# Attention and low-rank FFN on one core: the split of the softmax row sums between GpSimd and VectorE, 864/160 columns before, 896/128 after

## The reference

```python
x = x + layernorm(attention(layernorm(x)))     # 16 heads of 64 features, 2048 queries and keys
x = x + layernorm(ffn(layernorm(x)))           # x U1 (128x32), V1 (32x512) + b1, gelu, U2, V2 + b2
# attention, for every head:
q, k, v = x @ Wq + bq, x @ Wk + bk, x @ Wv + bv
out = softmax(q @ k.T / 8, axis=-1) @ v        # 2048 x 2048 probabilities a head
y = concat(out) @ Wo + bo
```

## Time and profile before

| | |
|---|---|
| median of three runs | 2367.11 us |
| the profiled execution | 2369.93 us, its span 2368.1 us |
| granted TensorE clock, mean | 0.991 of full speed |
| TensorE busy | 98% of the span |
| GpSimd busy | 92% |
| VectorE busy | 89% |
| ACT busy | 57% |
| DMA | 63.24 MB, 27 GB/s |

### The profile page before, as it was taken

One profiled execution on the slowest core, in us unless ns is written; L12 is line 12 of the kernel. 1 busy time (PEld: TensorE's weight loads), 2 busy tenths in 40 slices (PEclk: granted clock), 3 DMA queues, 4 the chain that ended last, 5 costly groups with the idle time before them and its releaser, 6 DMA issues.

```text
span 2368.1 us, 43238 instructions
## 1 busy us (share of the span) xinstructions
PE 2329.5 (98%) x15228; PEld 1191.7 (50%) x15228; DVE 2118.1 (89%) x3388; ACT 1355.7 (57%) x1610; POOL 2185.3 (92%) x1220
## 2 busy tenths in 40 slices
PE   8999999999999999999999999999999999999898
PEld 4455555555545555545555554554554555544444
DVE  7898999999999998999999999999999999888877
ACT  6655555555555656555555555555555565655545
POOL 6999999999999999999999999999999999989986
PEclk8999999999999999999999999999999999999998
DMA  2001001000000000100110000100000000110101
GB/s 60 25 17 29 29 15 33 29 15 28 29 19 28 29 24 19 33 27 17 29 31 17 28 29 15 33 29 15 28 29 21 27 29 24 27 33 24 37 23 36
DMA packets 88762, 63.24 MB, mean 27 GB/s; under 512 B 54661, under 2 KB 72453, under 8 KB 88549
## 3 DMA queue, kind: packets, MB, share of 16 engines
q1 hardware_dynamic: 87684, 60.21, 8.7%
q10 hardware_dynamic: 864, 0.26, 0.1%
HBM read 56.88 MB, written 2.61 MB: 25 GB/s over the span
## 4 chain that ended last, share of the span: by engine, by line
PE 90%; POOL 4%; DVE 3%; issue 1%; DMA 1%; ACT 1%; SPq 0%; POOLq 0%; DVEq 0%; ACTq 0%
PE o_ps L485 36%; PE spare_ps L440 14%; PE score_ps L464 10%; PE score_ps L470 9%; PE score_ps L467 9%; POOL total L1274 3%; PE spare_ps L408 3%; PE spare_ps L417 3%; PE spare_ps L426 3%; PE spare_ps L530 3%; DVE max_part L948 1%; DMA m_all<-m_scratch 1%; DVE ln_stats L920 0%; PE spare_ps L510 0%; SPq L1470 0%
## 5 line engine op out<-in xcount | busy, mean ns | idle before, releaser
L1274 POOL TENSOR_TENSOR total<-total,probs 128x864 f32<-128x864 f32 (+1 forms) x896 | 1822.1, 2034 | 142.7 <-ACT probs L757 32.7
L757 ACT ACTIVATE probs<-score_ps 128x1024 f32<-128x1024 f32 x1024 | 993.2, 1022 | 860.1 <-PE score_ps L470 860.1
L948 DVE TENSOR_REDUCE max_part<-spare_ps 128x1 f32<-128x512 f32 x2028 | 1294.9, 680 | 178.5 <-PE spare_ps L440 162.8
L485 PE MATMUL o_ps<-probs,v_sb 128*64 128x512 f32 x4096 | 982.1, 600 | 0.0
L485 PEld LDWEIGHTS o_ps<-probs,v_sb 128*64 128x64 f32 x4096 | 266.4, 137 | 447.6 <-issue 295.9
L440 PE MATMUL spare_ps<-k_hi,q_hi 64*128 64x512 f32 x2028 | 465.1, 451 | 10.8 <-DVE kd_lo L1133 5.6
L440 PEld LDWEIGHTS spare_ps<-k_hi,q_hi 64*128 64x128 f32 x2028 | 198.0, 184 | 463.3 <-issue 218.4
L464 PE MATMUL score_ps<-q_hi,kd_hi 64*128 64x512 f32 x2048 | 414.1, 398 | 5.1 <-ACT score_ps L747 5.1
L470 PE MATMUL score_ps<-q_hi,kd_lo 64*128 64x512 f32 x2048 | 408.6, 391 | 0.0
L467 PE MATMUL score_ps<-q_lo,kd_hi 64*128 64x512 f32 x2048 | 407.6, 390 | 0.0
L991 DVE TENSOR_REDUCE part_sum<-probs 128x160 f32<-128x640 f32 (+1 forms) x255 | 334.2, 1311 | 1.8 <-ACT probs L757 1.8
(11 more groups left out here) (150 smaller groups left out, 1268.4 us busy)
## 6 DMA issues: line engine op xcount, KB each, us to landing
m_all<-m_scratch SPq DMA_DIRECT2D x64, 512.0 KB, 3.6
denom<-denom_scratch SPq DMA_DIRECT2D x122, 128.0 KB, 2.9
m_scratch<-neg_rows SPq DMA_DIRECT2D x256, 1.0 KB
denom_quarters<-row_turned SPq DMA_DIRECT2D x224, 4.0 KB, 1.8
y_acc<-in_L_attn_x SPq DMA_DIRECT2D x8, 256.0 KB, 6.0
key_f<-in_L_attn_x SPq DMA_DIRECT2D x8, 256.0 KB, 3.0
block_out<-probs SPq DMA_DIRECT2D x8, 256.0 KB, 2.3
denom_scratch<-denom_col SPq DMA_DIRECT2D x61, 4.0 KB, 3.3
```

The costliest lines, as they stand in the source:

```text
L485: last = nc.tensor.matmul(o_ps[half(h), :], v_sb[:, b, kt, half(h)], probs[:, st % RING, h, :], start=(kt == 0), stop=(kt == T - 1))
L757: nc.scalar.activation(probs[:, st % RING], score_ps[st % 2][:], ACT.Exp, scale=SCALE).then_inc(s["exp_done"], 1)
L948: nc.vector.reduce_max(max_part[:, G % 2, h, qt, kc:kc + 1], bank[max_bank(n, h)], AX.X).then_inc(s["max_done"], 1)
L1274: nc.gpsimd.tensor_tensor(others(total[:, G % 2], G), so_far, others(probs[:, st % RING], G), ALU.add).then_inc(s["sum_done"], 1)
```

## The change

The constant that says how many of the 1024 columns VectorE takes goes from 160 to 128. So GpSimd adds 896 columns in each tile in place of 864, in chunks 0 to 62, and VectorE's reductions and merges of these chunks have 128 columns. The last chunk, the order of all instructions and all waits stay as they are.

```diff
-SHARE, GROUP = 160, 4
+SHARE, GROUP = 128, 4
```

## The result

The changed kernel takes 2411.88 us (median of four runs, 2409.80 to 2413.55). The kernel before takes 2365.67 us (median of four, 2364.19 to 2367.35). The ratio is 1.0200 with a 95% interval of 1.0185 to 1.0216, so the change costs 46.2 us, 2.0%. The forecast was 2414 us, with a range from 2400 to 2426.

A forecast was written before the change was run, and what follows sets the result against it. TensorE was taken to set the loop's pace, with GpSimd 99% taken and becoming the pace. 67.1 us of added adds, less 19.5 idle and 0.5 for VectorE, gave 47 us: 2414 us for the median, range 2400 to 2426.

The forecast's parts named there:

- GpSimd's reserve and the pace: Main loop: GpSimd has only 1.15 us a period to spare, so it becomes the pace at 143.6 us a period.
- The price of a column: GpSimd's adds: 32 more columns cost 0.071 us each, 67.1 us over 945 adds (bounds 56.7 to 71.4).
- The idle time taken up: GpSimd's present waits absorb 15.2 us in the loop and 4.3 us near the end, 19.5 together.
- Where TensorE is held: At output projection L530, TensorE waits for GpSimd's normalisation L1061, some 40 us in sum.
- The ring: Rival: only the eight probability tiles bind, exponentials waiting for adds; 9 us come free, 2405 us; 9%.
- VectorE's relief: Narrower reductions and merges take 72 us off VectorE's busy time, worth nothing for the end time except 0.5 us.
- The end: From chunk 59 to the last, the end moves with GpSimd, so the last chunks' growth counts in full.
- Start-up: GpSimd's wait ahead of the first add is start-up and takes up none of the added work.
- The sum: Whole kernel: 67.1 - 19.5 = 47.6 us, less 0.5 for VectorE, 47 us; 2414 us for the median.
- clock rival: TensorE's new waits lower its clock once a chunk: 56 us more, 2470 us; 7%.
- hidden: Rival: GpSimd's free time or shrinking gaps between adds absorb the whole 67.1 us, no change, 2367 us; 5%.
- VectorE: Rival: L440's waits for VectorE's maxima set TensorE's pace; at most 72 us come back, 2295 us; 4%.

The follow-up runs named there:

- 144: VectorE 144 columns, GpSimd 880, half of the change, against the kernel before (160/864): 16.0 us slower, ratio 1.0056 to 1.0084.
- gp_alone: GpSimd adds 896 columns as in the change, VectorE's four-tile reductions keep 160: 2409.50 us, 45.8 us slower than the kernel before.
- short_norm: The changed kernel with the normalisation L1061 multiplying only 8 of 512 columns: 2363.57 us against 2363.70 for the kernel before.
- late_projection: The changed kernel with output projection L530 in a chunk's fourth double step, not the second: 2410.70 us, 47.2 us slower than the kernel before.
- ve_alone: The kernel before with VectorE's four-tile reductions cut to 128 columns, GpSimd keeping 864: 2362.27 us against 2363.70.
- share152: VectorE 152 columns, GpSimd 872, against the kernel before (160/864): 1.1 us slower, ratio 0.9996 to 1.0018.
- late_share: The kernel before with 192/832 columns (VectorE/GpSimd) in chunks 56 to 62 only: 2361.87 us against 2363.50.
- 168: VectorE 168 columns, GpSimd 856, against the kernel before (160/864): 1.4 us slower, ratio 0.9999 to 1.0023.
- ve_norm_late: The changed kernel with VectorE doing L1061 to chunk 55, behind the second double step's maxima, and L530 in the fourth: 2502.97 us, 137.7 us slower than before.
- 192/832: VectorE 192 columns, GpSimd 832, against the kernel before (160/864): 14.3 us slower, ratio 1.0048 to 1.0078.
- ve_norm: The changed kernel with VectorE doing normalisation L1061 for chunks 0 to 55 in the same double step: 2543.71 us, 179.9 us slower than the kernel before.

## Why the prediction was right, and where it was off

*GpSimd's reserve and the pace.* Right. A reserve of 1.15 us a period was read, and the knee lies where it says: 1.15 us are 60 adds of 0.019 us, 9 columns, so between 152 and 151; 152 costs 1.1 us or nothing and 144 costs 16. Expected for 144 were 13 us. That it is GpSimd's time which costs is shown from two sides, by gp_alone and short_norm.

*The price of a column.* Right. 0.070 us was measured for 32 columns, 0.071 was taken, and 945 x 0.070 = 66.2 us. The working had a slip, though: it took the mean record of all 14 narrow adds, 1.617 us, as the length of the last of the four in the earlier trace rows. That one's own record is 1.553 us, which gives a start every 1.702 us and 0.0686 us for 32 columns, 64.8 us in all; the forecast would then have been 2 us lower. In the records the steps are 1970, 2040, 2109 and 2177 ns for 832 to 928 columns, 0.069 us each. The lower bound of 0.060 came from that same mean, into which three adds of 1.81 to 1.88 us go; with the median record of the 14, 1.553 us, the records give 0.070 us too. The Trainium skill (Perfetto Trace Analysis, GPSIMD Engine Instruction) says to treat the length of a GpSimd record as unreliable and to time by the spacing of starts. Here the spacing gave the better price, 67.1 us against 56.7, but the trace doesn't show the lengths to be off: between 864 and 896 columns both grow by 0.07 us. The mean had mixed disturbed adds with others.

*The idle time taken up.* Right in the loop: 15.2 us were there above the fixed 0.14 us a wait, and of these 1.7 - 4 x 0.143 = 1.1 us remain, where it waits for itself. The period came out at 143.5 us against 143.6.

*Where TensorE is held.* Right: 33.9 us at L530 behind L1061 (36.8 with the four that are booked on VectorE), where "some 40 us" were said. The ring isn't what binds. The page of waits does say that ACT waited for `total` 77.4 us in 36 places:

```profile
ACT probs L757 <- POOL total L1274: 77.4, 36, 2.2
...
1169.08 1.94 ACT L757 ACTIVATE probs<-score_ps 128x1024 f32<-128x1024 f32 x2 [3.65 <-PE score_ps L470]
1173.85 1.94 ACT L757 ACTIVATE probs<-score_ps 128x1024 f32<-128x1024 f32 x2 [2.15 <-POOL total L1274]
```

But the exponential at 1173.85 us is the chunk's seventh, and needs the add of eight tiles before, which is the previous chunk's and had been done before L1061 began at 1163.77 us. It waited for its scores: the last product into them, an L470, ended at 1173.42 + 0.39 = 1173.81 us. The name is that of an add that ended by chance at that time. In late_projection, of the same period, ACT has 896 us of waits for scores, and in the loop 3.1 us for `total`.

*VectorE's relief.* Right, at nothing for the end. The reductions lost 325.5 - 267.0 = 58.5 us and the merges 80.9 - 66.1 = 14.8 us, 73 in sum where 72 were worked out (the busy time of the page fell by only 56 us, as it counts adjoining records that overlap once). That ve_alone is no faster, and gp_alone no slower than the change, shows that it is worth nothing. VectorE does wait for `kd_lo` now, 5.8 us in 15 places, 0.4 each where 0.2 were said.

*The end.* The step that was too simple. It was assumed that the last chunks move with GpSimd in full. From the start of chunk 56 to the end of the span the change cost 1.9 us where 7 x 1.07 - 4.3 - 0.5 = 2.7 us were forecast. That is close, but one profile of each can't show it: this stretch took 352.4 us in the kernel before, but 348.4 and 349.4 us in ve_alone and share152, where GpSimd has the same adds or adds 8 columns wider; and it took 354.3 us in the change, but 356.6 us in gp_alone, which has the same adds. And late_share, which gives GpSimd 7 us there, returned 1.6. An end in which several engines in turn are at their limit would fit that, but it isn't shown. The twelve pieces of L931, for which up to 0.9 us were reckoned beside the sum, took 9.2 us in place of 9.1.

*Start-up.* No idle time was reckoned with there, so the first unit was to grow by 60 x 0.071 = 4 us. It grew by 2.3: TensorE's first wait for L1061 stands in the third chunk (1.6 us), and since it meets GpSimd at L530, behind the adds of the chunk before, the fourth chunk's growth shows only in the next unit.

*The sum.* 47 us forecast, 46.2 measured between medians, and 42.0 between the two profiled spans. Those two differ because the profiled run before, 2369.9 us, was itself 4.3 us above its median; the forecast took off 2.8 for it. The runs shown at first had a median of 2367.1 us, all four 2365.7; that is most of the 2 us by which 2414 was too high. That the sum came within 1 us is partly luck. From the first exponential to chunk 56 the profiles differ by 41.7 us, where 47 - 2.7 = 44.3 were forecast. If the rest of the 46.2 is the end's, that cost some 4.5 us and not 2.7, and the two errors cancelled in part.

*The clock rival* was wrong for waits of 0.7 to 1 us: PEclk stays 1.00 in all of the loop (188 to 2076 us). The *hidden* and the *VectorE* rivals fell with gp_alone and ve_alone. What gave a loss elsewhere, VectorE's wall at 192, was no part of the prediction; the expectation had it as one of three.

No share tried beats 160 by more than can be measured. 152 to 168 are one flat bottom, with a wall on each side.

## What to carry to other kernels

Read the reserve of an engine from its waits, not from its busy share: a chain of dependent instructions has a fixed gap in each link (0.14 us here, 7% of an add), and GpSimd at "92%" was 99% taken. Then look for the instruction at which the in-order leader meets that engine, and for its slack; with half a microsecond there, every further microsecond of the follower is a microsecond of the kernel. A spare share of an engine is worth something only at its place in the order: VectorE idled 12 us a period and had no room for a piece of 1.7 us ahead of its maxima. And a piece that is moved to another place has a price there of its own, 2.6 us a period for the projection, so a move is to be run without the change as well.

## What the runs showed of the hardware that was not expected

A VectorE product of two SBUF tiles beside GpSimd's adds took 0.691 us at best, 1.714 in the median, and 2.175 in the median where it always met one (adds of 2.1 us). Of the 56 products of ve_norm_late none was under 1.610 us and none over 2.615, and every one ended 0.55 us after the end of the add that was under way (0.546 to 0.554). The add behind it took 2.35 us in place of 2.1, so that the mean of all adds grew only from 2109 to 2120 ns. The Trainium skill (SBUF — State Buffer, Who interferes with whom) says that such an instruction contends with a GpSimd instruction that reads SBUF, that the lock is exclusive, and that the order of issue decides who is held up. The trace agrees: the product is held until the running add's end, whatever is left of it.

TensorE's busy share hid VectorE's pace in 192/832 wholly (141.56 of 141.60 us), since L440's records stretched by 10 ns in the mean.

And the clock answers to the size of a gap, not only to the sum. In the loop of ve_norm (188 to 2150 us) TensorE waited 104.2 us in 56 places, up to 2.8 us at a time, and the clock was at its lower level (1.2 GHz in place of 2.4) for 68 us. In that of ve_norm_late it waited 71.0 + 29.1 = 100.1 us in 92 places, up to 1.9 us, and the clock was there for 7 us. In the change, with gaps of up to 1.0 us, it never was. Each of the 17 falls in ve_norm stands at a gap of 2.0 to 2.8 us, but 21 more such gaps passed at full clock. TensorE's waits in ve_norm's loop, and two windows of it with one gap of 2.6 us each and the same busy time, one at full clock and one not:

```profile
PE spare_ps L440 <- DVE max_part L948: 104.2, 56, 2.8
...
400.00:440.00 40.00, 37.37 (x250) 19.26 (x248) 35.68 (x53) 20.88 (x24) 34.83 (x17) 1.00 0.10 28
...
560.00:600.00 40.00, 37.38 (x228) 18.43 (x226) 32.66 (x48) 20.04 (x23) 32.14 (x16) 0.91 0.08 21
```

Why one such gap brings the lower level and the next doesn't, the runs don't settle.
